# Loading three early operands on other queues and remaking the order tables of all engines in a two-layer FP32 kernel on Trainium2

## What is computed

```python
# layer 0: a linear map per sequence, then a mixture of 8 experts, the best 2 weighted by softmax
U = (mu @ W_dec + b_dec).reshape(B, 129, 30)
param = einsum('bik,kj->bij', U, V)            # 128x128 weight and a bias per sequence
xc = einsum('bsd,bde->bse', x, param[:, :-1]) + param[:, -1][:, None]
gate = xc @ Wg.T + bg;  w = softmax(top2(gate))
x = x + sum over the best 2 of w * (gelu(xc @ W1[e].T) @ W2[e].T + b2[e])
# layer 1: norms with gathered scales, a mixing MLP, then a gated MLP of width 512
h = ln(ln(x, pw[id]), cp[id]);  t = ln(x, tm[id]);  s = ln(x, ms[mask])
m, n, r = x + mlp_ln(three small states per sequence)
c = mlp_ln(concat(w0*h, w1*t, w2*m, w3*n, w4*r, w5*s))
g = silu(c @ w1.T * s1) * (c @ w2.T * s2)
g = gelu(g @ h1.T * t1);  g = gelu(g @ h2.T * t2)
x = x + g @ w3.T * s3
```

## Time and profile before

| | us |
|---|---|
| median of 3 runs | 433.73 (433.21 to 434.11) |
| the profiled execution | 432.91 |
| its span | 431.1 |

### The profile page before, as it was taken

One profiled execution on the slowest core, in us unless ns is written; L12 is line 12 of the kernel. 1 busy time (PEld: TensorE's weight loads), 2 busy tenths in 40 slices (PEclk: granted clock), 3 DMA queues, 4 the chain that ended last, 5 costly groups with the idle time before them and its releaser, 6 DMA issues.

```text
span 431.1 us, 5758 instructions
## 1 busy us (share of the span) xinstructions
PE 413.5 (96%) x1812; PEld 270.2 (63%) x1812; DVE 312.8 (73%) x656; ACT 292.0 (68%) x518; POOL 115.0 (27%) x122
## 2 busy tenths in 40 slices
PE   8698899999999999999999999999999999898996
PEld 5475455544656765776567665776577556677774
DVE  5489999987995587658866657678864788666653
ACT  4378967877756874677746884686668474857654
POOL 0026401443426520244153000448035031110000
PEclk9999999999999999999999999999999999999999
DMA  7976637563453342324531160325502210000000
GB/s 235 361 326 175 191 102 190 131 177 98 134 122 106 105 127 65 105 52 119 150 92 38 49 172 2 87 62 172 164 0 65 73 56 0 2 0 26 0 24 27
DMA packets 30216, 45.07 MB, mean 105 GB/s; under 512 B 3717, under 2 KB 22634, under 8 KB 29674
## 3 DMA queue, kind: packets, MB, share of 16 engines
q1 hardware_dynamic: 25504, 32.82, 26.4%
q0 software_dynamic: 3584, 10.49, 7.5%
q10 hardware_dynamic: 1098, 1.40, 1.1%
HBM read 40.68 MB, written 4.03 MB: 104 GB/s over the span
## 4 chain that ended last, share of the span: by engine, by line
PE 78%; DVE 9%; DMA 4%; issue 4%; ACT 3%; ACTq 1%; POOL 1%; SPq 1%; DVEq 0%
PE bank L750 21%; PE bank L648 20%; PE bank L786 7%; PE bank L696 7%; PE bank L640 6%; PE bank L735 5%; PE bank L664 2%; PE bank L703 2%; DMA keepP<-keepP_in 2%; DMA t_split<-tsS 2%; PE bank L775 1%; DVE mG L1190 1%; ACT mG L899 1%; PE bank L555 1%; DVE bn L1199 1%
## 5 line engine op out<-in xcount | busy, mean ns | idle before, releaser
L648 PE MATMUL bank<-mG,W 128*128 128x512 f32 x256 | 119.6, 593 | 0.0
L899 ACT ACTIVATE mG<-bank,keepP 128x512 f32<-128x512 f32 x128 | 85.3, 687 | 27.2 <-PE bank L640 17.6
L1464 POOL TENSOR_TENSOR rstd<-ve,mhalf 128x4 f32<-128x4 f32 x24 | 32.8, 1366 | 203.6 <-DVE ve L1205 203.5
L1190 DVE TENSOR_TENSOR mG<-mG,gwbs 128x1024 f32<-128x1024 f32 x64 | 77.3, 1218 | 2.1 <-DMA gwbs<-gate_w 1.3
L648 PEld LDWEIGHTS bank<-mG,W 128*128 128x128 f32 x256 | 47.5, 189 | 38.9 <-issue 35.3
L640 PE MATMUL bank<-ts,A 96*128 96x512 f32 x128 | 62.2, 526 | 1.7 <-ACT mG L899 1.6
L964 ACT ACTIVATE G<-bank,keepP 128x512 f32<-128x512 f32 x48 | 32.2, 692 | 27.9 <-PE bank L750 27.8
L1445 POOL DMA_INDIRECT gp<-pgb_in,ixall x32 | 35.8, 1119 | 26.7 <-issue 9.1
L750 PE MATMUL bank<-hB_h,h2w_h 128*128 128x512 f32 x96 | 39.7, 414 | 0.0
L750 PE MATMUL bank<-hA_h,h1w_h 128*128 128x512 f32 x96 | 38.7, 403 | 0.0
L1448 POOL DMA_INDIRECT gcm<-ctm,ixcm x32 | 35.1, 1098 | 9.8 <-issue 9.4
(11 more groups left out here) (243 smaller groups left out, 782.4 us busy)
## 6 DMA issues: line engine op xcount, KB each, us to landing
gwbs<-gate_w SPq DMA_DIRECT2D x32, 512.0 KB
keep<-xT_in SPq DMA_DIRECT2D x8, 256.0 KB, 6.0
outT<-keep SPq DMA_DIRECT2D x8, 256.0 KB, 2.1
t_split<-tsS SPq DMA_DIRECT2D x7, 192.0 KB
ts<-t_split SPq DMA_DIRECT2D x7, 192.0 KB
W1T<-W1T_in SPq DMA_DIRECT2D x1, 1024.0 KB, 8.7
W<-W2T_in SPq DMA_DIRECT2D x1, 1024.0 KB, 13.6
hs<-h1T_in SPq DMA_DIRECT2D x1, 1024.0 KB, 8.5
```

Of the source, the lines that this page charges most:

```text
L648: mm = pe.matmul(OACC[:, :], W2[:, e * HC + c, :], mG[n % NMG][:, c, :], start=False, stop=(e == E - 1 and c == HC - 1))
L899: act.activation(mG[e % NMG][:, c % HC, :], HM[n % 2][:, :], ACT.Gelu, bias=b1c[:, c:c + 1]).then_inc(m_gelu, 1)
L1190: dve.tensor_tensor(mine, mine, gate.unsqueeze(1).broadcast_to([P, HC, TT, P]), ALU.mult).then_inc(m_q, 1)
L1464: step(pool.tensor_tensor(rstd[:, n, :], ve[:, n, :], mhalf[:, :], ALU.pow))
```

## The change

Four things are changed.

1. **Queues.** `earlyP` goes out on SyncE's queue, between `keep[0]` and `W1T`, and no longer on ScalarE's. On ScalarE's queue `bdec` is third and `bdec_u` fourth, ahead of `wd_u`.
2. **Order tables.** All five tables are other ones, with the same steps; the numbers by which steps wait for the big weights' copies follow the new order of `wh` and `wl`.
3. **Products without readers.** There are five `fi` steps where there were four.
4. **The branch** stands after `H4` of the third stage, where it stood after `O2`, and the product `low` ahead of `O5` of the second stage.

```diff
@@ sync
             load(keep[0][:, :], A["xT"][:, 0:T], x_in[0])
+            load(earlyP[:, :], A["earlyP"], ld_small)
             load(W1T[:, :], A["W1T"], ld_W1T)
@@ scalar
             load(muT[:, :], A["cond_512T"].unsqueeze(1).broadcast_to([MU, 2, B]), ld_wd)
+            load(bdec, A["b_dec"][:, 0:KR * D].rearrange("o (i k) -> (o i) k", k=KR), ld_bd)
+            load(bdec_u, A["b_dec"][:, KR * D:KR * (D + 1)].rearrange("o k -> k o"), ld_bd)
             load(wd_u, A["W_dec"][:, KR * D:KR * (D + 1)].unsqueeze(1).broadcast_to([MU, 2, KR]), ld_wu)
-            load(bdec, A["b_dec"][:, 0:KR * D].rearrange("o (i k) -> (o i) k", k=KR), ld_bd)
             load(Vk[:, :], A["V"], ld_v)
             load(keepP[:, :], A["keepP"], ld_v)
-            load(earlyP[:, :], A["earlyP"], ld_small)
             act.wait_ge(setup0, 1)
             act.activation(warmA[:, 0:64], onesf[:, 0:64], ACT.Copy)
-            load(bdec_u, A["b_dec"][:, KR * D:KR * (D + 1)].rearrange("o k -> k o"), ld_bd)
@@ the tables, first line of TensorE's of each
-                (0, "A0 tm0 tm1 gm0 sq0 A1 A2 tm2 tm3 fi0 gx0 fi1 sq1 A3 tm4 tm5 gm1 gm2 fi2 H0 H1 fi3 H2 H3 H4 sq2 B H5 H6 O0 H7 "
+                (0, "A0 tm0 tm1 gm0 tm2 A1 sq0 A2 fi0 A3 fi1 gx0 gm1 tm3 tm4 sq1 gm2 H0 H1 fi2 H2 H3 fi3 tm5 fi4 gm3 B H4 H5 sq2 H6 "
...
-            eng.wait_ge(w_lo, max((4, 2, 1, 3)[n] for n in ns))
+            eng.wait_ge(w_lo, max((1, 4, 3, 2)[n] for n in ns))
...
-                dve.wait_ge(w_hi, (3, 1, 2, 4)[n])
+                dve.wait_ge(w_hi, (1, 3, 4, 2)[n])
```

More of the change, by code:

```diff
@@ L370, in build @@
                 (0, "tcl0 ix tcl1 tcl2 tab0 srt tab1 tab2 tab3 rt0"),
[L371 to L374, removed]
-                (5, "tab0 -rt0 tab1 tab2 =rt2 -rt1 -rt2 tab3 rt0 rt1"),
-                (6, "tab0 tab1 tab2 tab3"),
-                (7, "tab0 -rt0 -rt1 =rt2 tab1 tab2 -rt2 tab3 rt0 rt1 rt2"),
[7 rows of a table added]
             ),
             "SP": (
[8 rows of a table removed]
[8 rows of a table added]
             ),
```

## The result

| | us |
|---|---|
| before, median of 6 runs | 433.76 |
| after, median of 6 runs | 443.17 (441.85 to 444.9) |
| ratio | 1.0226 (95%: 1.0204 to 1.0247) |
| predicted | 429.3 (426.0 to 432.2) |
| the profiled execution of after, its span | 441.85, 440.0 |

A forecast was written before the change was run, and what follows sets the result against it. TensorE was taken to bound the middle, and the late-starting vector side the first two stages. Gains and losses of 4.0 - 0 - 0.5 + 0.9 = 4.4 us took the median from 433.73 to 429.3 us, range 426.0 to 432.2.

The forecast's parts named there:

- Part 1: Start, queues: TensorE's 3.88 us stop ahead of the 29th product goes; the chain behind moves 3.8 us earlier, `gm0` 3.7.
- Part 2: Tables at the start: first `q` at 38.7 us, 4.4 ahead on equal work; 4.0 carried to block 1's residual, range 1.5 to 6.5.
- the 4.4: Lead in us at VectorE's first `q`, on equal work, from a first gate search 4.0 us earlier and the new table.
- Rival B: Loads landing 2 us later, or ScalarE not keeping pace before the flag, give back 2.2 us: 431.5 us; chance 0.13.
- Part 3: Product without reader, `fi4`, ahead of `gm3`: costs TensorE about 0.86 us, hidden by the wait for `tcl3`.
- Part 4: Middle, same products reordered where TensorE has no idle time: a loss of 0.5 us, between 0 and 3.
- The sign that I had named for a wrong forecast: Idle time after the change in TensorE's full stretch, which had none from 150 to 200 us.
- Part 5: End: four `Fr2` products fill TensorE's 1.22 us wait ahead of a block 7 transpose; gain 0.9 us, 0 to 1.2.
- Rival D: Buffer loop of `keep` makes TensorE wait ahead of `XT` in blocks 3 to 5: 4 to 10 us, likeliest 434.8; chance 0.10.

The follow-up runs named there:

- q_only: Kernel before with its own order tables and only the change's queue orders for `earlyP`, `bdec` and `bdec_u`: 433.88 us, ratio 1.0002 to before.
- lr_late: `bu_early` with SyncE's load `lr` moved from directly behind `gb0` to behind `sts2`, `+lt` and `gb1`: 436.42 us, ratio 1.0079 to before.
- bu_early: Kernel before, its tables kept and `earlyP` left last on ScalarE's queue; only `bdec` and `bdec_u` go third and fourth: 430.67 us, ratio 0.9958.
- b_late: Changed kernel with `B` moved on TensorE from ahead of `H4` to ahead of block 0's first `O`: 440.9 us, ratio 1.0179 to before.
- lr_first: Changed kernel with SyncE's load `lr` moved directly behind `gb0`, ahead of `sts2`, `+lt` and `gb1`: 437.63 us, ratio 1.0116 to before.
- fixed3: `lr_first` with block 1's `O5` ahead of `Tt` and `low` on TensorE, and the queue order of `bu_early`: 436.51 us, ratio 1.0087 to before.

## Why the prediction was wrong

The forecast was 4.4 us less; it became 9.4 us more. By its own steps:

- **Part 1, the queues: half right.** The stop ahead of the 29th product went, with no half clock at 20 us, and `wd_u` (12.9) and `W1T` (10.4 after its issue, 13.2) landed as expected. The failing sentence is "from the 29th product on, everything that follows in the chain moves 3.8 us earlier". I followed the loads that the diff names and not those that stay: TensorE had waited only 0.30 us for `keepP` in before, at 12.61, and now it went out 0.7 us later, with `earlyP`'s 657.5 KB ahead of it on the other queue. 1.55 us were left in this profile, none in `q_only`. Nor did `tm1` wait for `keep[1]`: both `tm` ran through, and `gm0` waited 1.15 us for VectorE, with half clock behind it, a wait that I didn't have.
- **Part 2: the step that failed.** "The gates' way through DRAM starts some 3 us earlier as well and I price it at nothing" looked at the load that the first `q` waits for, `gb0`. The same way carries `lr`, for `B`. The new table moved it behind three other transfers, and I had the order of SyncE at hand. `lr_late` shows that this alone costs 5.2 us. So "I carry 4.0 of the 4.4" to the residual of block 1 failed: it came 7.3 us later, not 4.0 earlier. The carrying itself is sound in before's tables, where `bu_early` carries its 3.3 us to the end; what I left out is that TensorE has waits of its own on the way, and what the clock does behind them. The 4.4 failed too, ahead of that: `top0` began at 23.60, not 21.8, since part 1 fell short, and from there to the first `q` (41.55) it took 18.0 us, not 16.9; 0.46 of it is a wait for the gates' `tanh` on ScalarE.
- **Rival B had the second mechanism**, ScalarE and its followers out of step from 63 to 92 us, but priced it at 2.2 us of a gain; against before it cost 3.9 in after (lag 3.3 to 7.2). Which exchange of steps causes it stays open, and with it half of the 2.3%. Two corrections (`O5` ahead of `Tt`, `tc` behind `g15`) moved the waits on; the early test of the low parts is not what makes the lag grow from 65 to 82 us.
- **Part 3** was right about the size: 0.9 us for `fi4`. It was covered, by the wait ahead of `B`.
- **Part 4**, 0.5 us for the middle: the lag goes from 6.8 at 125 us to 7.6 at 394. About right. The sign that I had named for a wrong forecast, an idle time from 150 to 200 us, did come, with 0.72 us ahead of an `H` at 156.80 (TensorE busy 49.27 of 50), and it is a small part of the loss.
- **Part 5**, a gain of 0.9: three waits of 0.78, 1.22 and 1.11 became 0.78, 0.78 and 1.27, and a fourth of 0.31 is new (411.83), so the sum is as before, 3.1 us. The mechanism moved one wait; the gain was not there. That the lag grows by 0.9 from 394 us to the last product stays open.
- **Rival D**, the loss that I had looked for, is not there: no wait ahead of `XT` of blocks 3 to 6 shows in after, and TensorE is busy for 50.00 of 50 us from 200 to 250 and on to 350. The load of block 3 into `keep` was issued at 169.70 us, and `x` of block 3 ran at 173.69 without a wait.

## What to carry to other kernels

When an order is remade, follow the small loads, not the large ones: for each waiting step of the bounding engine look up which issue it waits for and what now stands ahead of that on its queue. A load of 48 KB issued 1.7 us later behind 896 KB held TensorE for 3.65 us, and with the clock that fell behind it the kernel took 5.2 us more. And of a load that is moved to another queue, ask for the small ones that stay: here 83 KB took 9.7 us to land instead of 8.0.

## What the runs showed of the hardware

The same stop does not always bring the clock down. In after and in `b_late` TensorE stood 2.66 us for `keepP` at the same place. In after the clock stayed at full (2.4 GHz) and the 16 products took 2.05 us; in `b_late` it was at 0.50 (1.2 GHz) from 17 to 19 us and they took 2.65:

```profile
14.97 0.21 PE L834 MATMUL bank<-keepP,Vk 30*128 30x30 f32 x1 [2.66 <-DMA keepP<-keepP_in]
15.11 2.65 PE L835 MATMUL bank<-muT,hs 128*128 128x128 f32 x16
17.69 0.63 PE L829 MATMUL bank<-muT,gap 128*30 128x128 f32 x2
```

Shorter ones don't always either. Behind the wait of 1.15 us ahead of `gm0` the clock is at 0.50 to 0.67 in after and `lr_first` (24 to 28 us) and at 0.50 in `fixed3` (24 to 30), but in `b_late` it stays full from 24 to 28. `lr_first`'s 1.70 us ahead of `Tt` has 0.62 and 0.52 behind it (82 to 86), and `fixed3`'s 1.71 us at the same work 1.00.

So executions of one kernel differ. After's six runs go from 441.85 us with a mean clock of 0.984 to 444.9 with 0.976, `bu_early`'s eight from 429.66 with 1.00 to 432.43 with 0.995. A difference of 2 to 3 us between two single profiles can be that alone.
